# A fused attention and feed-forward kernel on one core: the second half's feature rows transposed by TensorE instead of by DMA, and GpSimd's accumulating transfer issued later in each tile

## The chip, the core and the metric

The kernel runs on one NeuronCore of a Trainium2 chip. Its time is the device time of one execution in microseconds (us); lower is better. Engines are written as in the profile: PE is TensorE's matmuls, PEld its weight loads, DVE is VectorE, ACT is ScalarE, POOL is GpSimd, SP is SyncE, which only issues transfers.

## What is computed

The input `x` is 1024 rows (32 x 32) of 512 values. Cut to what matters:

```python
x = x + attention(conv(x) + context)      # 32 query heads, 8 key/value heads
m = mix(x)                                # per batch element a 32 x 32 mixing matrix and a bias
gate = silu(m @ dequant(gate_w))          # 512 -> 1792
up = m @ dequant(up_w)                    # 512 -> 1792
x = x + (gate * up) @ dequant(down_w)     # 1792 -> 512
```

The weights of the three last products are integers with a scale for each group of 128 rows and each column. The change touches only the feed-forward part, the last 180 us or so; what it calls features is `m`.

## The kernel before

**Stages.** First comes the convolution, then sixteen attention units (8 key/value heads x 2 halves of the rows), each with projections, scores and output products. All products are made in float16 from a high half and a low half of one operand or of both. Then comes the feed-forward part, in which everything is held transposed: channels on partitions, rows along the free axis.

**The feed-forward part.** The 1024 rows are two halves of 512 (`HT`), the 1792 inner channels are 14 blocks of 128 (`IC`). That gives `TILES` = 28 tiles, and tile `n` is block `n % 14` of half `n // 14`. In tile `n` PE runs `gate(n)` (4 banks, each a high and a low product, lines 1037 and 1038), `down(n-2, (0, 1))` (lines 1057 and 1061), `up(n)` (lines 1053 and 1054) and `down(n-2, (2, 3))`. That is 24 matmuls of 128x512 a tile; `down` runs two tiles behind (`LAG` = 2). The order is written out by hand, the same on every engine, and waits are on semaphore counts.

**The other engines in tile n.** ACT and DVE scale the banks of `gate` by the group's scale: ACT writes bank 0 into `whole` and bank 2 into `part`, DVE adds banks 1 and 3 (`scaled`, line 2021). POOL adds `part` to `whole` (`add_part`, line 2284), ACT takes silu of it (line 1447). ACT and DVE make `exact` out of the banks of `up` (lines 1467 and 2032). POOL multiplies (`hidden(n)`, line 2289), ACT makes the high half of the product (`hidden_high`, line 1476), POOL the low half (`hidden_low(n)`, line 2295), and `down(n)` on PE waits for the low half.

**The results of down.** Output blocks 0 and 2 of `down(n)` are added to `acc` by DVE (`down_added_to`, line 2054). Blocks 1 and 3 are scaled by ACT into one of three buffers `dprod` (line 1483), and one transfer issued by POOL adds both to `acc` in memory (`move_down(n)`, line 2307, 512 KB, for `n` = 1 to 24). `move_down(n)` first waits until `move_down(n-1)` has landed (`l_acc`), since both add to the same place. In the POOL program it stands after `hidden` and ahead of `add_part`:

```python
for n in range(LAG, TILES):
    if n > LAG:
        hidden(n - 1)
        move_down(n - 1 - LAG)
    add_part(n)
    hidden_low(n - 1)
```

**The residual.** `x` has to be transposed too. PE turns it in 8 groups of four 128x128 transposes into one bank, `side` (`turn_x`, line 1126): four for half 1 in tiles 9 to 12 (`TURN_X`), copied by ACT into `acc`, and four for half 0 in tiles 16 and 17. The latter DVE adds to half 0's finished `acc` (`result(c)`, line 2071), and SP stores them. `result(1)` waits for the landing of `move_down(13)`, the last of half 0. It stands on DVE between the two `scaled` of tile 17, and `turn_x(0, 2)` on PE waits for it, because it reuses `side`.

**The features.** Half 0's features are transposed by PE at the start of the part. Half 1's are computed during tiles 2 to 4 into `fnat` (4 tiles of 128 rows, rows on partitions). In tiles 5, 7, 9 and 11 (`ROWS`) ACT makes the high half and DVE the low half of one row tile in `fpair` (`rows_high`, line 1429; `rows_low`, line 2013), still with rows on partitions. SP then issues 16 transposing transfers (line 654) into `fT`, which `gate(14)` reads.

**The bound of the hidden values.** For each half a maximum over partitions is broadcast: PE transposes (`hidden_rows`, line 1002), DVE reduces (line 1992) and multiplies a 4x4 identity with it (line 1993, `hdiag`), PE multiplies `spread` with that (`hidden_all`, line 1008). For half 1 it is done in tiles 5 and 6.

**The end.** After the loop `down` of tiles 26 and 27 follows (`last_downs`), DVE adds 6 blocks, of which the first, block 3 of tile 25, waits for the landing of `move_down(24)`, then `hidden_low(27)` and the others; POOL adds four blocks (`add_down`, line 2319), the first of which waits for the same landing.

## Time and profile before

| | us |
|---|---|
| median of 3 executions (lowest, highest) | 681.24 (680.61, 681.83) |
| the profiled execution, its own time | 680.94 |
| its span, first to last instruction | 679.1 |
| PE busy in it | 659.5 |
| DVE, POOL, ACT busy in it | 563.2, 458.5, 411.9 |
| first matmul of the feed-forward part | 500.0 |

The granted TensorE clock is 0.997 on average, which is the 2.4 GHz level. A matmul row of 128x512 is listed with 0.38 us, but the next one starts 0.216 us later; for the pace of PE one reads the distance between starts. In the timeline a row is: start, duration, engine, line, operation, output<-inputs, shape, count, and in brackets how long the engine had been idle before and who ended that.

### The profile page before, as it was taken

What the parts mean: (1) busy time and instruction counts of PE and PEld (TensorE: products, weight loads), DVE (VectorE), ACT (ScalarE), POOL (GpSimd) and SP (SyncE); (2) the same over time, 40 slices, a digit from 0 to 9 for tenths busy, and PEclk for the clock granted to TensorE, in tenths of its full rate; (3) what the DMA queues carried; (4) which work ended last, traced back from release to release, by engine and by line L of the source; (5) the groups of instructions that cost most, each with busy time, mean ns of one, the idle gap of its engine ahead of it and who ended that gap; (6) DMA issues with size and microseconds to landing.
All of it is one profiled execution on the core that took longest, in us unless ns stands there. A gap on an engine that the chain in (4) does not pass through costs nothing.

```text
span 679.1 us, 14435 instructions
## 1 busy us (share of the span) xinstructions
PE 659.5 (97%) x4952; PEld 370.0 (54%) x4952; DVE 563.2 (83%) x870; ACT 411.9 (61%) x1233; POOL 458.5 (68%) x379
## 2 busy tenths in 40 slices
PE   9998999999999999999999999999989999999995
PEld 8855555646566465665656656565644434444441
DVE  4979779879879788987978888777785999899997
ACT  0477663845647384374655638446475778877874
POOL 0367973884685497288659648747537678887886
PEclk9999999999999999999999999999999999999998
DMA  7520157379359348536735943563300156556454
GB/s 262 189 95 1 66 163 140 94 178 183 104 100 270 94 90 268 104 89 158 203 85 106 278 109 77 160 106 102 57 1 0 32 109 124 110 110 139 94 105 113
DMA packets 112672, 82.70 MB, mean 122 GB/s; under 512 B 93264, under 2 KB 93936, under 8 KB 110448
## 3 DMA queue, kind: packets, MB, share of 16 engines
q1 hardware_dynamic: 108736, 69.51, 40.4%
q0 software_dynamic: 3456, 12.58, 9.9%
q8 instruction: 24, 0.39, 0.2%
q14 instruction: 24, 0.20, 0.1%
q10 hardware_dynamic: 432, 0.01, 0.0%
HBM read 48.14 MB, written 2.21 MB: 74 GB/s over the span
## 4 chain that ended last, share of the span: by engine, by line
PE 75%; DVE 8%; POOL 7%; issue 4%; DMA 3%; ACT 2%; SPq 1%; POOLq 0%; DVEq 0%; ACTq 0%
PE bank L677 19%; PE bank L679 18%; PE bank L678 18%; PE bank L1053 2%; PE bank L1054 2%; PE bank L1037 2%; PE bank L1061 2%; PE bank L1038 2%; PE bank L1057 2%; DMA acc<-dprod 2%; POOL wqlo L2156 2%; PE bank L877 1%; DMA wqr<-in_wq 1%; DVE mx L1594 1%; DVE exact L2032 1%
## 5 line engine op out<-in xcount | busy, mean ns | idle before, releaser
L677 PE MATMUL bank<-wohi,oThi 128*128 128x512 f16 x256 | 97.1, 379 | 2.2 <-DVE oTlo L1802 2.1
L677 PE MATMUL bank<-wqhi,cThi 128*128 128x512 f16 x256 | 97.0, 379 | 0.8 <-POOL wqlo L2156 0.6
L678 PE MATMUL bank<-wolo,oThi 128*128 128x512 f16 x256 | 97.0, 379 | 0.0
L679 PE MATMUL bank<-wohi,oTlo 128*128 128x512 f16 x256 | 97.0, 379 | 0.0
L679 PE MATMUL bank<-wqhi,cTlo 128*128 128x512 f16 x256 | 97.0, 379 | 0.0
L678 PE MATMUL bank<-wqlo,cThi 128*128 128x512 f16 x256 | 97.0, 379 | 0.0
L1222 ACT ACTIVATE qraw<-bank 128x512 f32<-128x512 f32 x64 | 37.9, 592 | 82.4 <-PE bank L679 82.1
L2166 POOL TENSOR_TENSOR wolo<-wor,wohi 128x512 f16<-128x512 f32 x32 | 42.6, 1353 | 57.9 <-ACT wohi L1202 57.9
L2204 POOL TENSOR_TENSOR qinv<-qms,neghalf 128x8 f32<-128x8 f32 x28 | 53.6, 1914 | 39.3 <-ACT qms L1241 39.3
L1233 ACT ACTIVATE qsq<-qraw 128x128 f32<-128x128 f32 x256 | 75.5, 302 | 1.7
L677 PE MATMUL bank<-wkvhi,cThi 128*128 128x256 f16 x256 | 69.9, 273 | 0.0
L678 PE MATMUL bank<-wkvlo,cThi 128*128 128x256 f16 x256 | 69.8, 273 | 0.0
L679 PE MATMUL bank<-wkvhi,cTlo 128*128 128x256 f16 x256 | 69.8, 273 | 0.0
L2192 POOL TENSOR_TENSOR qn<-qraw,down 128x512 f16<-128x512 f32 x56 | 66.9, 1195 | 2.8 <-ACT qraw L1222 2.8
L2032 DVE SCALAR_TENSOR_TENSOR exact<-bank,uscl,exact 128x512 f32<-128x512 f32 x84 | 62.7, 747 | 7.2 <-ACT exact L1467 2.9
L2156 POOL TENSOR_TENSOR wqlo<-wqr,wqhi 128x512 f16<-128x512 f32 x32 | 43.3, 1382 | 27.0 <-ACT wqhi L1188 27.0
L1810 DVE SCALAR_TENSOR_TENSOR x<-bank,ysc,x 128x512 f32<-128x512 f32 x64 | 46.1, 743 | 16.3 <-PE bank L679 16.2
L2289 POOL TENSOR_TENSOR whole<-whole,exact 128x512 f32<-128x512 f32 x27 | 36.5, 1350 | 21.4 <-DVE exact L2032 20.2
L1233 ACT ACTIVATION_READ_ACCUMULATOR qsq<-qraw 128x1 f32 x256 | 49.5, 193 | 0.0
L1202 ACT ACTIVATE wohi<-wor 128x512 f16<-128x512 f32 x32 | 17.5, 618 | 48.3 <-DVE wor L1622 48.3
L1759 DVE SCALAR_TENSOR_TENSOR qn<-qraw,qn 128x512 f16<-128x512 f32 x56 | 41.5, 751 | 5.2 <-POOL qn L2192 4.9
L1053 PE MATMUL bank<-fT,uint 128*128 128x512 f16 x112 | 42.5, 380 | 1.7 <-DVE whole L2021 1.4
(231 smaller groups left out, 1806.6 us busy)
## 6 DMA issues: line engine op xcount, KB each, us to landing
acc<-dprod POOLq DMA_DIRECT2D x24, 512.0 KB, 4.6
wqr<-in_wq SPq DMA_DIRECT2D x8, 1024.0 KB, 7.4
wor<-in_wo SPq DMA_DIRECT2D x8, 1024.0 KB, 9.2
raw<-in_gu_w SPq DMA_DIRECT2D x28, 256.0 KB, 3.5
zeros<-in_gu_z SPq DMA_DIRECT2D x28, 256.0 KB, 4.6
wkvr<-in_wkv SPq DMA_DIRECT2D x8, 512.0 KB, 7.2
raw<-in_dn_w SPq DMA_DIRECT2D x14, 256.0 KB, 2.8
zeros<-in_dn_z SPq DMA_DIRECT2D x14, 256.0 KB, 3.5
```

The source lines that it names most:

```text
L677: mm(o, ahi, bhi, start=start and k == 0, stop=False)
L678: mm(o, ahi, blo, start=False, stop=False)
L679: last = mm(o, alo, bhi, start=False, stop=stop and k == n - 1)
L1053: mm(o, uint[:, i, c, :], fThi[:, c, tokens(half)], start=True, stop=False)
L1233: A(qsq[:, t % 2, g, :], qraw[:, t, g, :], ACT.Square, accum_out=qss[:, g, t:t + 1]).then_inc(a_qss, 1)
L1759: V.scalar_tensor_tensor(qpair[:, t, 1, :, :], qraw[:, t, :, :], V_DOWN, qpair[:, t, 0, :, :], ALU.mult, ALU.subtract).then_inc(d_qlo, 1)
L1810: V.scalar_tensor_tensor(x[:, q, :], PC[t][:, :], ysc[:, half:half + 1], x[:, q, :], ALU.mult, ALU.add).then_inc(d_y, 1)
L2032: V.scalar_tensor_tensor(u, up_bank(n, c)[:, :], uscl[:, half, i, c:c + 1], u, ALU.mult, ALU.add).then_inc(d_us, 1)
L2156: Q.tensor_tensor(wqlo[:, c, :], wqr[:, c, :], wqhi[:, c, :], ALU.subtract).then_inc(p_wq, 1)
L2166: Q.tensor_tensor(wolo[:, g, :], wor[:, g, :], wohi[:, g, :], ALU.subtract).then_inc(p_wo, 1)
L2192: Q.tensor_tensor(qpair[:, t, 0, :, :], qraw[:, t, :, :], down[:, :, None].broadcast_to([P, G, HD]), ALU.mult).then_inc(p_qhi, 1)
L2204: Q.tensor_tensor(qinv[:, :, pair], qms[:, :, pair], neghalf[:, :, pair], ALU.pow).then_inc(p_qpow, 1)
```

## The change

It does four things.

1. The four row tiles of half 1's features are transposed by PE from `fnat` (float32) into `side`, by a new function `turn_rows`, in tiles 7, 8, 10 and 12 (`ROWS`). ACT and DVE make the halves out of that bank, straight into `fT`. The 16 transposing transfers of SP and the buffer `fpair` are gone; `gate(14)` waits for DVE's last low half instead.
2. `turn_x` of half 1 moves from tiles 9 to 12 to tiles 9, 11, 13 and 14. The bank `side` is now shared, so each group waits for the reader of the group before.
3. In POOL's loop `move_down(n - 3)` stands behind `hidden_low(n - 1)` instead of ahead of `add_part(n)`, but in the last tile it stays ahead. Its waits are the same.
4. `hdiag` is gone: DVE only reduces, and PE multiplies the broadcast row maximum with the identity. ACT's copy of the result in tile 7 stands earlier.

```diff
-ROWS = (5, 7, 9, 11)
-TURN_X = (9, 10, 11, 12)
+ROWS = (7, 8, 10, 12)
+TURN_X = (9, 11, 13, 14)
...
-            for t in range(HQ):
-                sp.wait_ge(d_fTlo, KC + t + 1)
-                for b in range(BQ):
-                    start = HT + P * t + S * b
-                    sp.dma_start(fT[:, :, :, start:start + S].rearrange("p k c n -> p (k c) n"),
-                                 fpair[S * b:S * b + S, t, :, :, :].rearrange("p k c n -> p (k c) n"),
-                                 transpose=True).then_inc(l_fT, 16)
...
-                pe.wait_ge(d_hdiag, half + 1)
+                pe.wait_ge(d_hrow, half + 1)
...
-                mm(bound_all(), spread[0:MAXIMA, :], hdiag[0:MAXIMA, :], start=True, stop=True).then_inc(t_hx, 1)
+                mm(bound_all(), hrow[0:MAXIMA, :].broadcast_to([MAXIMA, P]), ident[0:MAXIMA, 0:MAXIMA],
+                   start=True, stop=True).then_inc(t_hx, 1)
...
-                        pe.wait_ge(l_fT, 16 * HQ * BQ)
+                        pe.wait_ge(d_fTlo, KC + HQ)
...
-                elif c:
+                elif c == 3:
                     pe.wait_ge(a_xT, c)
                 else:
                     pe.wait_ge(d_y, HQ * UNITS)
-                    pe.wait_ge(a_hm, 2)
+                    pe.wait_ge(d_fTlo, KC + c + 2)
...
+            def turn_rows(t):
+
+                pe.wait_ge(a_fnat, HQ + t + 1)
+                if t == 0:
+                    pe.wait_ge(a_hm, 2)
+                elif t == 1:
+                    pe.wait_ge(d_fTlo, KC + t)
+                else:
+                    pe.wait_ge(a_xT, t - 1)
+                for c in range(KC):
+                    last = nc.tensor.transpose(side[:, P * c:P * c + P], fnat[:, t, P * c:P * c + P], ident)
+                last.then_inc(t_rows, 1)
...
-                    turn_x(1, n - TURN_X[0])
+                    turn_x(1, TURN_X.index(n))
+                elif n in ROWS:
+                    turn_rows(ROWS.index(n))
...
-                act.wait_ge(a_fnat, HQ + t + 1)
-                A(fpair[:, t, 0, :, :], fnat[:, t, :].rearrange("p (c n) -> p c n", n=P), ACT.Copy,
+                act.wait_ge(t_rows, t + 1)
+                A(fThi[:, :, rows(t)], side[:, :].rearrange("p (c n) -> p c n", n=P), ACT.Copy,
...
-                V.scalar_tensor_tensor(fpair[:, t, 1, :, :], fnat[:, t, :].rearrange("p (c n) -> p c n", n=P), fup[:, 1:2],
-                                       fpair[:, t, 0, :, :], ALU.mult, ALU.subtract).then_inc(d_fTlo, 1)
+                V.scalar_tensor_tensor(fTlo[:, :, rows(t)], side[:, :].rearrange("p (c n) -> p c n", n=P), fup[:, 1:2],
+                                       fThi[:, :, rows(t)], ALU.mult, ALU.subtract).then_inc(d_fTlo, 1)
...
             for n in range(LAG, TILES):
                 if n > LAG:
                     hidden(n - 1)
+                if n == TILES - 1:
                     move_down(n - 1 - LAG)
                 add_part(n)
                 hidden_low(n - 1)
+                if LAG < n < TILES - 1:
+                    move_down(n - 1 - LAG)
```

The instruction order of the two kernels at the three places that the prediction speaks of follows. Line numbers of the changed kernel differ a little from those before (POOL: 2295 is `add_part`, 2300 `hidden`, 2306 `hidden_low`, 2318 `move_down`).

POOL, tiles 25 to 27 before (2289 is `hidden`, 2284 `add_part`, 2295 `hidden_low`, 2307 `move_down`, 2319 `add_down`), from `hidden(25)` on:

```order
L2289 TENSOR_TENSOR whole<-whole,exact 128x512
L2307 DMA acc<-dprod 128x1024
L2284 TENSOR_TENSOR whole<-whole,part 128x512
L2295 TENSOR_TENSOR hT<-whole,hT 128x512
L2289 TENSOR_TENSOR whole<-whole,exact 128x512
L2307 DMA acc<-dprod 128x1024
L2284 TENSOR_TENSOR whole<-whole,part 128x512
L2295 TENSOR_TENSOR hT<-whole,hT 128x512
L2319 TENSOR_TENSOR acc<-acc,dprod 128x512 x4
```

POOL at the same place of the changed kernel:

```order
L2300 TENSOR_TENSOR whole<-whole,exact 128x512
L2295 TENSOR_TENSOR whole<-whole,part 128x512
L2306 TENSOR_TENSOR hT<-whole,hT 128x512
L2318 DMA acc<-dprod 128x1024
L2300 TENSOR_TENSOR whole<-whole,exact 128x512
L2318 DMA acc<-dprod 128x1024
L2295 TENSOR_TENSOR whole<-whole,part 128x512
L2306 TENSOR_TENSOR hT<-whole,hT 128x512
L2330 TENSOR_TENSOR acc<-acc,dprod 128x512 x4
```

`move_down(23)` has moved behind two compute instructions, `move_down(24)` has stayed, and only `hidden(26)` is left between them. In tiles 4 to 26 the pattern is that of the first four rows.

DVE before, from the end of tile 5 into tile 6 (2013 is `rows_low`, 1992 and 1993 the reduction and `hdiag`, 2021 `scaled`):

```order
L2054 SCALAR_TENSOR_TENSOR acc<-bank,dsc,acc 128x512
L2032 SCALAR_TENSOR_TENSOR exact<-bank,uscl,exact 128x512
L2013 SCALAR_TENSOR_TENSOR fpair<-fnat,fup,fpair 128x512
L1992 TENSOR_REDUCE hrow<-bank 4x1
L1993 SCALAR_TENSOR_TENSOR hdiag<-const,hrow 4x4
L2021 SCALAR_TENSOR_TENSOR whole<-bank,gscl,whole 128x512
```

DVE at the same place of the changed kernel:

```order
L2065 SCALAR_TENSOR_TENSOR acc<-bank,dsc,acc 128x512
L2043 SCALAR_TENSOR_TENSOR exact<-bank,uscl,exact 128x512
L2006 TENSOR_REDUCE hrow<-bank 4x1
L2032 SCALAR_TENSOR_TENSOR whole<-bank,gscl,whole 128x512
L2032 SCALAR_TENSOR_TENSOR part<-bank,gscl,part 128x512
```

Two instructions have left the stretch ahead of tile 6's first `scaled`; `rows_low` stands in tile 7 for the first time.

PE in the changed kernel, in the middle of tile 7 (1054 and 1058 are `down`, 1136 is `turn_rows`, 1050 and 1051 are `up`):

```order
L1054 MATMUL bank<-hT,dints 128x512
L1058 MATMUL bank<-hT,dints 128x512
L1136 MATMUL bank<-const,fnat 128x128 x4
L1050 MATMUL bank<-fT,uint 128x512
L1051 MATMUL bank<-fT,uint 128x512
```

Before there was nothing between `down` and `up` in tiles 7, 8, 13 and 14, and `turn_x` in tiles 9 to 12; now each of the tiles 7 to 14 has one group of four transposes there.

## Rows read from the trace of the kernel before

**Rows 1.** The page, part 1: busy us (share of the span) and instructions.
```profile
PE 659.5 (97%) x4952; PEld 370.0 (54%) x4952; DVE 563.2 (83%) x870; ACT 411.9 (61%) x1233; POOL 458.5 (68%) x379
```

**Rows 2.** Timeline of PE, first matmuls of tiles 15 and 16.
```profile
597.14 0.38 PE L1037 MATMUL bank<-fT,gint 128*128 128x512 f16 x1
...
602.32 0.38 PE L1037 MATMUL bank<-fT,gint 128*128 128x512 f16 x1
```

**Rows 3.** Timeline of PE, tile 6: its first matmul, a stall in `up`, tile 7's first.
```profile
544.54 0.38 PE L1037 MATMUL bank<-fT,gint 128*128 128x512 f16 x1
...
547.35 0.38 PE L1054 MATMUL bank<-fT,uint 128*128 128x512 f16 x1
548.78 0.39 PE L1053 MATMUL bank<-fT,uint 128*128 128x512 f16 x1 [1.05 <-DVE whole L2021]
...
551.13 0.38 PE L1008 MATMUL bank<-hdiag,spread 4*128 4x4 f32 x2
551.45 0.39 PE L1037 MATMUL bank<-fT,gint 128*128 128x512 f16 x1
```

**Rows 4.** Timeline of DVE, end of tile 5 and start of tile 6.
```profile
546.18 0.74 DVE L2013 SCALAR_TENSOR_TENSOR fpair<-fnat,fup,fpair 128x512 f16<-128x512 f32 x1
546.84 0.27 DVE L1992 TENSOR_REDUCE hrow<-bank 4x1 f32<-4x128 f32 x1
547.14 0.92 DVE L1993 SCALAR_TENSOR_TENSOR hdiag<-const,hrow 4x4 f32<-4x4 f32 x1
547.99 0.73 DVE L2021 SCALAR_TENSOR_TENSOR whole<-bank,gscl,whole 128x512 f32<-128x512 f32 x1
```

**Rows 5.** Timeline of PE, a group of transposes in tile 9.
```profile
564.78 0.60 PE L1126 MATMUL bank<-const,x 128*128 128x128 f32 x4
565.21 0.38 PE L1053 MATMUL bank<-fT,uint 128*128 128x512 f16 x1
```

**Rows 6.** Timeline of PE, a stall in tile 14.
```profile
591.68 0.38 PE L1038 MATMUL bank<-fT,gint 128*128 128x512 f16 x1
593.22 0.39 PE L1057 MATMUL bank<-hT,dints 128*128 128x512 f16 x1 [1.16 <-POOL hT L2295]
```

**Rows 7.** Chain of waits, 580 to 594 us: start, us, what.
```profile
582.81 6.51 DMA acc<-dprod
...
589.87 0.04 POOL acc L2307
```

**Rows 8.** The page, part 6: POOL's transfers, KB each, median us to landing.
```profile
acc<-dprod POOLq DMA_DIRECT2D x24, 512.0 KB, 4.6
```

**Rows 9.** Timeline of POOL, tile 16: `move_down(13)`, `add_part(16)`, `hidden_low(15)`.
```profile
605.52 0.88 POOL L2307 DMA_DIRECT2D acc<-dprod  x1
606.14 1.57 POOL L2284 TENSOR_TENSOR whole<-whole,part 128x512 f32<-128x512 f32 x1
607.38 1.45 POOL L2295 TENSOR_TENSOR hT<-whole,hT 128x512 f16<-128x512 f32 x1
```

**Rows 10.** Timeline of DVE: the second `scaled` of tile 16, and `result(1)` in tile 17.
```profile
605.11 0.74 DVE L2021 SCALAR_TENSOR_TENSOR part<-bank,gscl,part 128x512 f32<-128x512 f32 x1
...
610.52 0.68 DVE L2071 TENSOR_TENSOR acc<-bank,acc 128x512 f32<-128x512 f32 x1
```

**Rows 11.** Timeline of PE, tile 17: its first matmul, and `turn_x(0, 2)`.
```profile
608.38 0.38 PE L1037 MATMUL bank<-fT,gint 128*128 128x512 f16 x1
...
611.35 0.63 PE L1126 MATMUL bank<-const,x 128*128 128x128 f32 x4 [0.22 <-DVE acc L2071]
```

**Rows 12.** Timeline of POOL from `hidden_low(25)` to the end.
```profile
661.77 1.45 POOL L2295 TENSOR_TENSOR hT<-whole,hT 128x512 f16<-128x512 f32 x1
664.32 1.28 POOL L2289 TENSOR_TENSOR whole<-whole,exact 128x512 f32<-128x512 f32 x1 [1.10 <-DVE exact L2032]
665.54 0.88 POOL L2307 DMA_DIRECT2D acc<-dprod  x1
...
670.18 5.76 POOL L2319 TENSOR_TENSOR acc<-acc,dprod 128x512 f32<-128x512 f32 x4 [1.35 <-DMA acc<-dprod]
```

**Rows 13.** Busy time by stretch; columns: us, busy PE, PEld, DVE, ACT, POOL, PEclk, DMA share, GB/s.
```profile
673.00:679.00 6.00, 0.10 (x1) 0.00 (x0) 2.38 (x4) 0.17 (x1) 2.66 (x3) 0.67 0.47 175
```

More of the change, by code:

```diff
@@ L262, in build @@
         between = sb("between", [P, 5 * DM + 40], F32, ffn)
-        fpair = sb("fpair", [P, HQ, 2, KC, P], F16, ffn)
+        between2 = sb("between2", [P, HQ, 2, KC, P], F16, ffn)
         dprod3 = sb("dprod3", [P, 2, HT], F32, ffn)
@@ L393, in build @@
         d_fTlo = sem("d_fTlo")
-        l_fT = sem("l_fT")
+        t_rows = sem("t_rows")
         t_g = sem("t_g")
@@ L408, in build @@
         d_hx = sem("d_hx")
-        d_hdiag = sem("d_hdiag")
+        d_hrow = sem("d_hrow")
         t_hx = sem("t_hx")
@@ L461, in tokens, with rows @@
             return slice(HT * half, HT * half + HT)
+        def rows(t):
+            return slice(HT + P * t, HT + P * t + P)
         def up_bank(n, c):
@@ L1525, in _ @@
                 scaled(n, 2)
+                if n == 7:
+                    hidden_scale(1)
                 if n >= LAG:
@@ L1533, in _ @@
                     rows_high(ROWS.index(n))
-                if n == 7:
-                    hidden_scale(1)
-                elif n in TURN_X:
-                    turned_x(n - TURN_X[0])
-                elif n == IC - 1:
+                if n in TURN_X:
+                    turned_x(TURN_X.index(n))
+                if n == IC - 1:
                     later_scales()
@@ L1988, in hidden_bound, with hidden_maxima @@
                 V.tensor_reduce(hx[:, 0:1], fmx[:, half, 0:HQ], AX_X, ALU.max).then_inc(d_hx, 1)
-            def hidden_diagonal(half):
+            def hidden_maxima(half):
                 dve.wait_ge(t_hx, 2 * half + 1)
-                link(V.tensor_reduce(hrow[0:MAXIMA, :], bound_rows(half), AX_X, ALU.max))
-                V.scalar_tensor_tensor(hdiag[0:MAXIMA, :], ident[0:MAXIMA, 0:MAXIMA], TOP,
-                                       hrow[0:MAXIMA, :].broadcast_to([MAXIMA, MAXIMA]), ALU.mult,
-                                       ALU.mult).then_inc(d_hdiag, 1)
+                if half:
+                    dve.wait_ge(t_hx, 2)
+                V.tensor_reduce(hrow[0:MAXIMA, :], bound_rows(half), AX_X, ALU.max).then_inc(d_hrow, 1)
             def hidden_power(half):
@@ L2078, in _ @@
             mix_power(0)
-            hidden_diagonal(0)
+            hidden_maxima(0)
             probs_low(UNITS - 1)
@@ L2102, in _ @@
                 elif n == 6:
-                    hidden_diagonal(1)
+                    hidden_maxima(1)
                 elif n == 9:
```

## The prediction, made before the changed kernel ran

> **What bounds the kernel now.** I read the page first: PE is busy for 97% of the span [rows 1]. So the sum has to be made of PE's time: what instructions it gains or loses, and where it waits. Next I read the timeline of PE in the feed-forward part, since the change touches nothing ahead of it except one small DVE instruction. The pace is the distance between the first matmuls of two tiles. In tile 15, which has nothing but its 24 matmuls, it is 602.32 - 597.14 = 5.18 us [rows 2], and that is 24 times 0.216. This is the floor of a tile. Then I looked for the tiles that are longer than the floor plus their extra instructions, and asked at each what came last:
>
> - Tile 6 takes 551.45 - 544.54 = 6.91 us. In `up` PE stands still from 547.35 to 548.78, 1.21 us more than the normal distance, and DVE's `scaled` releases it [rows 3]. DVE is late because `rows_low`, the reduction and `hdiag` stand ahead of that `scaled`, from 546.18 to 547.99 [rows 4].
> - Tile 14 has a stall of 593.22 - 591.68 - 0.22 = 1.32 us, released by POOL's low half [rows 6]. The chain of waits says why: a transfer of `move_down` took 6.51 us to land instead of the median 4.6 [rows 7, 8], POOL could issue the next only at 589.87, and `add_part` and `hidden_low` stood behind it. SP's transposing transfers were under way at that time.
>
> From tile 6 to tile 14 PE spends 597.14 - 544.54 = 52.60 us [rows 2, 3].
>
> **The change, part by part.**
>
> *Transposes on PE, and the stalls they replace.* A group of four float32 transposes moves the next matmul by 565.21 - 564.78 = 0.43 us [rows 5]. Half 1's residual groups are only moved within tiles 7 to 14; four groups are new, +1.72 us. After the change each of the tiles 7 to 14 has exactly one group. If no stall is left, tiles 6 to 14 take 9 x 5.18 + 8 x 0.43 = 50.06, and the broadcast product at tile 6's end keeps its 551.45 - 551.13 = 0.32 [rows 3]: 50.38 us, or 2.2 less than the 52.60 of before. So this part **gains 2.2 us net**: 1.7 paid, 3.9 of stalls removed (1.2 in tile 6, 1.3 directly in tile 14, the rest small ones, also from late row halves and late transfers). Does it really leave no stall? Three things have to hold.
>
> First, tile 6: without `rows_low` and `hdiag` the `scaled` can start when the reduction ends, at 546.18 + 0.3 instead of 547.99, and done 0.7 later it is ahead of PE's demand at 547.57. Second, DVE in a row tile has 8 large instructions at the pace of 0.66 us (546.18 to 546.84 [rows 4]), 5.3 us; a tile now lasts 5.18 + 0.43 = 5.61, so DVE does not fall behind, which it did when row tiles had no group on PE. Third, the shared bank: in tiles 8, 9, 11 and 13 PE waits for the DVE part of the group before. DVE ends it 546.84 - 544.54 = 2.3 us after the next tile's first matmul [rows 3, 4]; PE wants the bank after 12 matmuls, 12 x 0.216 = 2.6 us. It is just in time, by 0.3 us. I cost it at nothing; if the cover is gone, up to 0.5 at each of four places.
>
> ACT and DVE make the same number of halves as before, from the bank instead of from memory; DVE's `scaled`, which reads a bank, is listed with 0.73 us and `rows_low` with 0.74 [rows 4], so this costs nothing. SP has nothing else to do while it issues the 16 transfers, so their removal frees no one but the DMA queues. `hdiag` of half 0 stands in a chain of DVE work at 498 us ahead of `gate(0)`; I take 0.15 us off for it, between 0 and the 0.9 of rows 4.
>
> *`move_down` behind the low half.* On POOL `add_part` and `hidden_low` no longer stand behind the issue (605.52 to 606.14 [rows 9], 0.62 us) and its wait. PE paces all tiles, so that is worth only the stalls counted above. But the transfer now starts later, and the landing has readers. Most have tiles of slack: the next `move_down` has a tile of 5.18 us against 4.6 of landing plus 0.54 until POOL goes on (582.81 + 6.51 = 589.32, issue at 589.87 [rows 7]), 5.14 in all, which just fits. Two readers have none.
>
> (a) *Tile 17.* `result(1)` waits for the landing of `move_down(13)`. Before it was issued at 605.52 [rows 9] and landed 4.6 later [rows 8], at 610.1; DVE came to `result(1)` at 610.52 [rows 10], 0.4 us after it. Now the order is `add_part(16)`, `hidden_low(15)`, then the transfer. `add_part(16)` cannot start before DVE's `scaled` of tile 16 ends, 605.11 + 0.74 = 605.85 [rows 10]. It takes 607.38 - 606.14 = 1.24 [rows 9], so the low half starts at about 607.15. The low half takes between 1.24 (the same size) and its listed 1.45. The transfer is issued at 608.4 to 608.6 and lands at 613.0 to 613.2. `result(1)` starts 2.5 to 2.7 us later than before, and so does `turn_x(0, 2)` on PE, which was already released by it with 0.22 us of idle [rows 11]. Behind it PE's `up(17)` is queued, behind `result(1)` on DVE the second `scaled` of tile 17. Everything shifts, and as later tiles are at the floor nothing gives it back: **+2.6 us**.
>
> (b) *The end.* `move_down(24)` keeps its place, but waits for `move_down(23)`, which is now issued behind `hidden_low(25)`. That started at 661.77 [rows 12] and can be at most 0.15 earlier; with 1.24 to 1.45 for it the issue is at 662.9 to 663.2, the landing 4.6 later at 667.5 to 667.8, and POOL goes on 0.54 later, at 668.0 to 668.3 instead of 665.54 [rows 12]: 2.4 to 2.8 us. Queued behind it are `add_part(27)` and `hidden_low(26)`, for which PE's last `down` waits, and its landing, for which DVE's first added block and POOL's first of four adds wait, at 670.18 before. The four adds took 5.76 us though 4 x 1.27 = 5.1 would do, so up to 0.4 can come back. I take **+2.3**, bounds 1.9 and 2.8.
>
> How a page stands to that: the Trainium skill (DMA: Bandwidth & Descriptors, the two cost components) fits a transfer's time as 2.0 us plus its bytes at 436 GB/s. For 512 KB that would be an estimated 3.2 us, and the two waits would come out 1.3 us shorter each. The trace disagrees, the median row is 4.6 for this accumulating transfer, and the sum goes by the row.
>
> *Sum.* -2.2 - 0.15 + 2.6 + 2.3 = +2.55 us. The profiled execution of before took 680.94, so 683.5 by its own time; the median of the runs, 681.24, is 0.3 above it, and I give **683.8 us** for the median.
>
> **The rivals.** A measurement of this kernel can tell about 0.2% from no change: 1.36 us, so "same" is 679.9 to 682.6.
>
> 1. *Faster: the later landings are never waited for.* Then only -2.35 is left, 678.9 us. It decides at tile 17: the landing must be there by 610.5 in the old timeline, so the issue by 605.9. But the low half ahead of it starts at 607.15 by rows 9 and 10. Only if POOL's chain ran much ahead of DVE could it be, and DVE's `scaled` binds it. Chance 0.06.
> 2. *Only one of the two waits is paid in full*, because a slack I did not see takes the other, or both land about 1.2 us sooner. Then -2.35 + 2.5 gives about 681.4, no change. For it: SP's transfers are gone, which stretched landings to 6.51. Against it: the median was undisturbed already. Chance 0.13.
> 3. *The shared bank.* The row part on DVE comes after PE's demand at four places. With 0.3 to 0.5 us each that is 1.2 to 2.0 more: 685.0 to 685.8. The margin is 0.3 us, but DVE was late there before for a cause that is removed. Chance 0.07.
> 4. *The clock.* In tile 17 PE now stands still for 0.4 + 2.6 = 3 us, twice its longest pause in this part. After its last matmul the mean granted clock of the last 6 us is 0.67 [rows 13], so it does fall to the 1.2 GHz level when PE has no work. Were it to fall in tile 17, each following tile would take 10.4 instead of 5.18 as long as it lasts: 686 or more. Chance 0.04. The Trainium skill (TensorE: Matmul & The Clock Gate, why this matters for your kernels) warns that idle gaps of PE in mid-kernel can bring it back to the lower clock. The trace shows pauses of up to 1.3 us [rows 6] without that and no longer one, so it stays a small chance.
>
> **How the numbers follow.** The forecast has 0.70, on its own 682.9 to 684.8 by the bounds of (a) and (b) and 0.5 for what I leave out. The range has to take in most of rival 2 and the start of rival 3: 681.2 to 685.3 leaves out rival 1, part of 2 and 3, and 4, some 0.18. Slower by over 0.2% is the forecast but for its low edge (0.68), rivals 3 and 4: 0.79 with rounding. Same is rival 2 and that edge, 0.14. Faster is rival 1 and a little more, 0.07.
>
> **What would show it.** In the changed profile: no stall in `up` of tile 6; 5.61 us a tile from 7 to 14, and about 50.4 us from tile 6's to tile 15's first matmul; four new groups of 0.43. In tile 17 a gap on PE of some 3 us ahead of `turn_x(0, 2)`, behind it DVE's `result(1)` with about 2.5 us of idle time that ends with a DMA landing. In the last tile POOL idle for about 2.4 us ahead of `move_down(24)`, released by the DMA. I am wrong if `result(1)` has no idle time, if the last `move_down` is issued within 1 us of the end of `hidden(26)`, or if tiles 8, 9, 11 and 13 are longer than 5.7 us.

## The result, and the profile after

The change makes the kernel slower: 687.04 us (686.72 to 687.99) against 681.34 us of the kernel before, a ratio of 1.0072 with the interval 1.0044 to 1.01. The forecast was 683.8 us, its range ended at 685.3. The direction was right, the size was not. (The ratios here and in the table below are those of the measurement; the quotient of two medians can differ from them by about 0.1%.) The rest speaks of the profiled execution of after, 686.72 us with a span of 684.9, beside before's span of 679.1: 5.8 us more.

The page after, answering to [rows 1] (PE's busy time, and the granted clock in 40 slices, whose last one is 7 tenths, before 8):

```profile
PE 662.8 (97%) x4968; PEld 374.6 (55%) x4968; DVE 562.0 (82%) x868; ACT 413.6 (60%) x1233; POOL 456.7 (67%) x379
...
PEclk9999999999999999999999999999999999999997
```

PE's busy share is 97% as before, so the loss must be looked for by stretches. Busy time by windows, for after; the windows are tile 6 to tile 14, tiles 15 and 16, tile 17 in two pieces, tiles 18 to 26, and the end:

```profile
core 0: us, PE busy (x) PEld busy (x) DVE busy (x) ACT busy (x) POOL busy (x), PEclk, DMA share, GB/s
545.56:596.32 50.76, 50.76 (x252) 24.65 (x250) 46.52 (x72) 43.61 (x76) 41.54 (x41) 1.00 0.50 94
596.32:607.56 11.24, 11.24 (x58) 5.64 (x57) 10.60 (x17) 9.17 (x16) 9.41 (x9) 1.00 0.54 107
607.56:613.72 6.16, 2.75 (x15) 1.10 (x12) 2.90 (x5) 2.51 (x4) 2.32 (x3) 0.95 0.51 107
613.72:618.57 4.85, 4.85 (x21) 2.71 (x22) 3.73 (x6) 1.96 (x4) 2.86 (x3) 0.71 0.29 110
618.57:665.19 46.62, 46.62 (x219) 21.13 (x217) 42.84 (x64) 39.06 (x63) 39.55 (x36) 1.00 0.55 108
665.19:684.90 19.71, 10.74 (x41) 4.08 (x39) 12.82 (x18) 7.00 (x12) 11.39 (x10) 0.82 0.43 107
```

The same three stretches of before (tiles 6 to 14, tile 17, the end):

```profile
544.54:597.14 52.60, 50.04 (x236) 22.27 (x234) 47.37 (x73) 42.59 (x74) 43.15 (x41) 1.00 0.60 110
608.38:614.84 6.46, 6.24 (x35) 3.21 (x33) 5.88 (x10) 4.60 (x8) 4.96 (x5) 1.00 0.72 175
661.99:679.10 17.11, 9.66 (x41) 3.49 (x39) 12.87 (x19) 7.33 (x12) 11.07 (x10) 0.88 0.45 115
```

That gives the account of the 5.8 us:

| stretch | before | after | difference | forecast |
|---|---|---|---|---|
| up to tile 6's first matmul | 544.54 | 545.56 | +1.02 | -0.15 |
| tiles 6 to 14 | 52.60 | 50.76 | -1.84 | -2.2 |
| tiles 15 and 16 | 11.24 | 11.24 | 0 | 0 |
| tile 17 | 6.46 | 11.01 | +4.55 | +2.6 |
| tiles 18 to 26 | 47.15 | 46.62 | -0.53 | 0 |
| the end | 17.11 | 19.71 | +2.60 | +2.3 |

**Tile 17.** PE's timeline answers to [rows 11]: it stands still 3.57 us longer than the normal 0.22 from one start to the next (609.93 to 613.72), and behind that its matmuls come 0.43 us apart instead of 0.22 until 616.30.

```profile
609.93 0.38 PE L1058 MATMUL bank<-hT,dints 128*128 128x512 f16 x1
613.72 1.08 PE L1123 MATMUL bank<-const,x 128*128 128x128 f32 x4 [3.41 <-DVE acc L2082]
614.60 0.63 PE L1050 MATMUL bank<-fT,uint 128*128 128x512 f16 x1
615.02 0.63 PE L1051 MATMUL bank<-fT,uint 128*128 128x512 f16 x1
...
616.30 0.48 PE L1050 MATMUL bank<-fT,uint 128*128 128x512 f16 x1
616.62 0.38 PE L1051 MATMUL bank<-fT,uint 128*128 128x512 f16 x1
```

A spacing twice as long is the 1.2 GHz level; the granted clock of that window was 0.71. It costs 0.45 in the transposes (0.88 instead of 0.43) and 0.94 in the five matmul distances from 614.60 to 616.62 (2.02 instead of 1.08): 1.39 us. DVE and POOL show who is waited for, as in [rows 9, 10]: `result(1)` waits for a landing, and that transfer was issued at 608.22.

```profile
612.88 0.69 DVE L2082 TENSOR_TENSOR acc<-bank,acc 128x512 f32<-128x512 f32 x1 [3.15 <-DMA acc<-dprod]
```

```profile
603.15 0.88 POOL L2318 DMA_DIRECT2D acc<-dprod  x1 [1.02 <-DMA acc<-dprod]
603.76 1.58 POOL L2300 TENSOR_TENSOR whole<-whole,exact 128x512 f32<-128x512 f32 x1
605.00 1.58 POOL L2295 TENSOR_TENSOR whole<-whole,part 128x512 f32<-128x512 f32 x1
606.45 1.24 POOL L2306 TENSOR_TENSOR hT<-whole,hT 128x512 f16<-128x512 f32 x1
608.22 0.88 POOL L2318 DMA_DIRECT2D acc<-dprod  x1 [0.53 <-ACT dprod L1495]
```

`move_down(12)` was issued at 603.15, not because of the low half, but because it waited for the landing before it, and landed at 607.68. POOL issued the next 0.54 later. The low half in front of it ended at the same moment, 606.45 + 1.24 = 607.69.

**The end.** POOL's timeline answers to [rows 12]. Its first add comes at 675.97, before at 670.18, 5.79 later, of which 3.20 were there at the last tile's first matmul (665.19 against 661.99) and 2.59 are new. From that add to the end of the span it is 8.93 us, before 8.92, so PE's lower clock in this stretch (0.82, before 0.88) costs nothing here.

```profile
666.26 0.88 POOL L2318 DMA_DIRECT2D acc<-dprod  x1 [0.44 <-ACT dprod L1495]
667.18 1.27 POOL L2300 TENSOR_TENSOR whole<-whole,exact 128x512 f32<-128x512 f32 x1
671.33 0.88 POOL L2318 DMA_DIRECT2D acc<-dprod  x1 [2.88 <-DMA acc<-dprod]
671.93 1.56 POOL L2295 TENSOR_TENSOR whole<-whole,part 128x512 f32<-128x512 f32 x1
673.15 1.45 POOL L2306 TENSOR_TENSOR hT<-whole,hT 128x512 f16<-128x512 f32 x1
675.97 5.75 POOL L2330 TENSOR_TENSOR acc<-acc,dprod 128x512 f32<-128x512 f32 x4 [1.37 <-DMA acc<-dprod]
```

### The profile page after: what moved, and what is told of

Read it like the earlier page. It is cut to its first block and busy times, and to the rows that moved or that the text cites. A ratio compares the mean times of both kernels' runs of the same rounds, so it can differ in the third digit from the quotient of the medians.

```text
span 684.9 us, 14456 instructions
## 1 busy us (share of the span) xinstructions
PE 662.8 (97%) x4968; PEld 374.6 (55%) x4968; DVE 562.0 (82%) x868; ACT 413.6 (60%) x1233; POOL 456.7 (67%) x379
## 5 line engine op out<-in xcount | busy, mean ns | idle before, releaser
L1495 ACT ACTIVATE dprod<-bank,dsc 128x512 f32<-128x512 f32 x52 | 35.7, 686 | 18.1 <-PE bank L1058 17.0
L1058 PE MATMUL bank<-hT,dints 128*128 128x512 f16 x112 | 42.5, 388 | 3.3 <-POOL hT L2306 3.3
```

Of the source, the lines that this page charges most:

```text
L1058: mm(down_bank(n, c)[:, :], dints[:, n % IC, P * c:P * c + P], hTlo[:, n % (LAG + 1), :], start=False, stop=True).then_inc(t_dn, 1)
```

## The experiments

Theory A says that the place of `move_down` costs all of the loss, by two waits for a landing and by the clock behind the first. Its rivals are: the transposes on PE; POOL's order itself rather than the landings; another cause of the low clock. Each comparison stands beside runs of the kernel before on the same chip, whose median was 681.34 to 681.9 us.

| run | us | ratio to before | 95% interval |
|---|---|---|---|
| changed kernel | 687.04 | 1.0072 | 1.0044 to 1.01 |
| `move_down` in the old place | 678.87 | 0.9962 | 0.9946 to 0.9979 |
| before, new place alone | 690.5 | 1.0123 | 1.0091 to 1.0154 |
| old place in tile 16 only | 687.53 | 1.0073 | 1.0044 to 1.0101 |
| old place in tile 26 only | 688.48 | 1.0098 | 1.0068 to 1.0127 |
| pause filled with matmuls | 684.35 | 1.0037 | 1.0024 to 1.0051 |
| half the bytes | 679.79 | 0.9964 | 0.9945 to 0.9983 |
| between add and low half | 688.68 | 1.01 | 1.0084 to 1.0116 |
| half 0's results a tile later | 682.3 | 1.0 | 0.9986 to 1.0015 |
| before, without `hdiag` | 680.41 | 0.9965 | 0.9947 to 0.9983 |
| old place, results later | 679.73 | 0.9971 | 0.9953 to 0.9989 |
| results later, old place from tile 18 | 681.37 | 0.9991 | 0.9974 to 1.0009 |

**The old place, with all the rest of the change.**

```diff
                 if n > LAG:
                     hidden(n - 1)
-                if n == TILES - 1:
+                if n > LAG:
                     move_down(n - 1 - LAG)
                 add_part(n)
                 hidden_low(n - 1)
-                if LAG < n < TILES - 1:
-                    move_down(n - 1 - LAG)
```

> The changed kernel with `move_down` back in its old place (right behind `hidden`, ahead of `add_part`) in every tile; the transposes on PE, the missing `hdiag` and the rest stay. Theory A (the two waits on late landings, and the clock that fell behind the first, cost all of it): no gap over 1 us on PE in tile 17, POOL goes on with the last transfer without a wait of 2.9 us, tiles 6 to 14 stay at about 50.8 us; the time is the changed kernel's less 4.5 and less 2.6, 679.9 us, 1.2 to 1.8 below the kernel before. Theory B (the transposes on PE and the shared bank cost the time): the time stays above 684. Theory C (without the new place the low half is late in the tiles 6 to 14): stalls of 1 us come back there and the time is 681 to 682.

Measured: 678.87 us, 0.38% below before. The windows of tiles 6 to 14, tile 17 and the end of this run:

```profile
544.36:595.12 50.76, 50.76 (x252) 24.61 (x250) 46.53 (x72) 43.59 (x76) 41.47 (x41) 1.00 0.50 95
606.36:612.76 6.40, 6.24 (x34) 3.20 (x32) 6.18 (x11) 4.58 (x8) 4.93 (x5) 1.00 0.72 176
661.93:679.20 17.27, 9.49 (x41) 3.57 (x39) 12.64 (x18) 7.33 (x12) 11.02 (x10) 0.91 0.44 112
```

Theory A holds and B falls: tiles 6 to 14 are as quick as in after, tile 17 and the end as short as before. C falls too, the low half is not late in tiles 6 to 14. So the parts of the change that gain are those on PE and DVE, and the new place costs 1.0072 - 0.9962 = 1.1%, 7.5 us.

The old place is not free, though. The profiled execution was the slowest of the twelve, 681.05 us, and in it tile 26 takes 7.26 us, 2.08 more than the floor: POOL waited for a landing of 6.7 us (issued at 647.42), the add and the low half stood behind that wait, and PE waited for the low half. The same happened in tile 14 of before; here no transposing transfer was under way.

```profile
654.68 0.88 POOL L2318 DMA_DIRECT2D acc<-dprod  x1 [2.03 <-DMA acc<-dprod]
656.53 1.44 POOL L2306 TENSOR_TENSOR hT<-whole,hT 128x512 f16<-128x512 f32 x1
658.03 0.39 PE L1054 MATMUL bank<-hT,dints 128*128 128x512 f16 x1 [1.47 <-POOL hT L2306]
```

**The new place alone.** The kernel before, on POOL:

```diff
                 if n > LAG:
                     hidden(n - 1)
+                if n == TILES - 1:
                     move_down(n - 1 - LAG)
                 add_part(n)
                 hidden_low(n - 1)
+                if LAG < n < TILES - 1:
+                    move_down(n - 1 - LAG)
```

> The kernel before with one part of the change alone: `move_down(n - 3)` behind `hidden_low(n - 1)`, the last tile excepted. Theory A: tile 17 takes 9.5 to 11 us with a gap of over 3 us on PE, with the clock at its lower level behind it, and the last tile is about 2.5 us longer: 681.3 + 4.5 + 2.5 = 688.3 us, less up to 1.3 for the stall of tile 14, so 687 to 688.5. Theory B (the waits need the transposes on PE to become long): 681 to 683.

Measured: 690.5 us, slower than the changed kernel and above what either theory gave. The two long tiles are there (10.34 us and an end of 20.92), and a third one that I had not foreseen, tile 9 with 9.39 us. POOL's and DVE's timelines there (POOL first):

```profile
564.53 0.88 POOL L2307 DMA_DIRECT2D acc<-dprod  x1 [1.35 <-DMA acc<-dprod]
565.14 0.50 POOL L2345 TENSOR_TENSOR ht<-hm 128x1 f32<-128x1 f32 x1
565.71 0.19 POOL L2347 TENSOR_TENSOR ht<-ht 128x1 f32<-128x1 f32 x1
565.98 0.19 POOL L2349 TENSOR_TENSOR ht<-ht,hm 128x1 f32<-128x1 f32 x1
...
566.21 0.15 DVE L2001 TENSOR_SCALAR hdown<-ht 128x1 f32<-128x1 f32 x1 [2.65 <-POOL ht L2349]
```

`hidden_product(1)` stands behind tile 8's `move_down` on POOL. That waits for a landing of 5.3 us, beside SP's transposing transfers, and DVE's `hidden_power(1)`, with all of DVE's queue behind it, waits for the product. PE then stood still for 2.3 us and its clock fell there as well (0.84 over the tile). In the changed kernel the transposing transfers are gone and tile 9 takes 5.85. The two parts of the change so depend on each other: the new place is worse with the old transfers.

**One tile's place alone, 16 or 26.** The condition of the first, and of the second:

```diff
-                if n == TILES - 1:
+                if n in (IC + LAG, TILES - 1):
                     move_down(n - 1 - LAG)
...
-                if n == TILES - 1:
+                if n >= TILES - 2:
                     move_down(n - 1 - LAG)
```

with the tiles named left out of the condition behind `hidden_low`.

> The changed kernel with `move_down(13)` alone, in tile 16, ahead of `add_part`. Theory A1 (the low half and the add in front of that one transfer make it late, as the prediction had it): it is issued at about 605, lands at 610, tile 17 takes 6.5 us and the time is 687.0 - 4.5 = 682.5. Theory A2 (the chain of transfers makes it late: in the changed kernel the landing of `move_down(12)` came at 607.68 and POOL went on 0.54 later): it is issued at 608.2 as before, POOL's `add_part(16)` and `hidden_low(15)` now stand behind it, PE's gap in tile 17 keeps its 3.8 us and the time is 687 or up to 1.5 more.

> The changed kernel with `move_down(23)` alone, in tile 26, ahead of `add_part`. Theory A1 (its own place makes the end late): it is issued at about 664.9 instead of 666.3, lands at 669.5, the last `move_down` follows 1.3 us sooner, and with it the four adds: 687.0 - 1.3 = 685.7. Theory A2 (the whole chain of transfers since tile 17 runs one issue late: `move_down(22)` landed at 665.72): the issue is at 666.26 in any case, `add_part(26)` and `hidden_low(25)` come behind it, and the time stays within 0.5 us of 687.0 or gets longer.

Measured: 687.53 and 688.48 us, no gain from either. POOL in tile 16 of the first:

```profile
602.86 0.88 POOL L2318 DMA_DIRECT2D acc<-dprod  x1 [1.05 <-DMA acc<-dprod]
603.47 1.59 POOL L2300 TENSOR_TENSOR whole<-whole,exact 128x512 f32<-128x512 f32 x1
607.93 0.88 POOL L2318 DMA_DIRECT2D acc<-dprod  x1 [2.87 <-DMA acc<-dprod]
608.53 1.56 POOL L2295 TENSOR_TENSOR whole<-whole,part 128x512 f32<-128x512 f32 x1
```

A2 holds in both. In the first the transfer is issued where it was, 0.55 us after the landing before it; moved forward it only makes the add and the low half wait too, and PE stands still in two places (2.3 and 1.4 us). In the second `move_down(23)` is bound by the landing before it in the same way (POOL idle for 2.46 us ahead of the issue at 665.10), and PE stands still for 2.1 us in the last tile for the low half. Its profiled execution, 685.54 us, was the fastest of six, and its time alone would have spoken for A1. This corrects my reason for (a): the low half in front of the one issue (in after it ended at 607.69, the landing came at 607.68) is not the only thing that makes it late; a chain of transfers in which each waits for the last does it by itself. The second profile shows this without a stretched landing: the transfer before was issued at 660.00, so the moved one could not come ahead of 665.10, and at the new place it would have come only some 0.1 us later (an estimate: the two issues before lie 5.24 us apart). One link takes 4.53 + 0.54 = 5.07 us of a tile's 5.18. A stretched landing, such as the 5.85 us of the transfer issued at 596.76, is given back at 0.1 us a tile (0.5 in a row tile). At the old place the chain runs two POOL instructions earlier, 1.27 for the add and 1.24 for the low half, so it can be 2.5 us ahead of where it is now, and that is the reserve that the change gave away.

**The pause filled.** In tile 17, ahead of `turn_x`:

```diff
                 elif n in (IC + LAG, IC + LAG + 1):
+                    if n == IC + LAG + 1:
+                        pe.wait_ge(a_g, 2 * n + 1)
+                        for _ in range(15):
+                            mm(up_bank(n, 0)[:, :], uint[:, n % IC, 0, :], fThi[:, 0, tokens(1)], start=True, stop=True)
                     turn_x(0, 2 * n - 2 * IC - 2 * LAG)
```

> The changed kernel with 15 more matmuls on PE in tile 17 (15 x 0.216 = 3.24 us), in front of `turn_x(0, 2)`, so that PE works through most of the pause of 3.57 us; their product lands in the bank that `up(17)` overwrites afterwards, so nothing of the result changes. The waits stay as they are. Theory A (the pause lets the clock fall, and that costs 1.4 us behind it): no low clock behind tile 17, distances of 0.22 us in `up(17)` at once, tile 17 takes 9.6 us instead of 11.0 and the time is 687.0 - 1.4 = 685.6. Theory B (the low clock in tile 17 has another cause): it comes in this tile all the same, PE does the 15 matmuls and the time is 687 or above.

Measured: 684.35 us, though PE does 3.2 us more work. Its timeline, with the fillers in one row:

```profile
609.70 3.40 PE L1173 MATMUL bank<-fT,uint 128*128 128x512 f16 x15
613.21 0.63 PE L1123 MATMUL bank<-const,x 128*128 128x128 f32 x4
613.68 0.38 PE L1050 MATMUL bank<-fT,uint 128*128 128x512 f16 x1
613.89 0.38 PE L1051 MATMUL bank<-fT,uint 128*128 128x512 f16 x1
```

The clock stays up (1.00 over the tile), the tile takes 9.59 us instead of 11.01, 1.42 less. That is theory A, by the two profiles: with the pause filled the clock does not fall, and its fall cost 1.4 of the 4.55 us; the wait cost the other 3.15. The median fell by 2.7, more than this tile, but the two intervals overlap (1.0024 to 1.0051 and 1.0044 to 1.01); in the profiled execution it was 0.45 earlier already at tile 17's first matmul, and its end was 0.5 shorter.

**Half the bytes.**

```diff
-                    pool.dma_start(acc[:, half, 2:KC, :],
-                                   moved_blocks(n)[:, :, :], accum_op=ALU.add).then_inc(l_acc, 16)
+                    pool.dma_start(acc[:, half, 2:3, :],
+                                   moved_blocks(n)[:, 0:1, :], accum_op=ALU.add).then_inc(l_acc, 16)
```

> The changed kernel with half of each accumulating transfer left out: 256 KB, block 2 of the down product, where 512 KB with blocks 2 and 3 were moved; block 3's sums of 24 tiles are missing from the result. Landing bounded by 2.3 (half of 4.5) and 4.5 us; I take 3.3. Theory A (what is waited for is the landing): `result(1)` and the last `move_down` wait about 1.2 us less each, and each next transfer has 1.2 us of slack, so that a stretched one no longer makes the next one late; tile 17 takes 8 to 9.5 us, the end is 1.2 to 2.4 shorter, in all 682.5 to 684.5. Theory B (POOL's order alone, add and low half ahead of the issue, costs it, whatever is moved): 686.5 to 687.5.

Block 3 of the down product is left out of the transfers, so the result is not the kernel's. Measured: 679.79 us, faster than before and below what either theory gave, with POOL's order unchanged. The median landing came after 3.3 us. `result(1)` still waits, but 1.22 us instead of 3.15, and the last `move_down` 1.14 instead of 2.88. PE's pause in tile 17 is 1.6 us and the clock stays up; tile 17 takes 7.72 us, the end 17.06. B is refuted. I had put the gain too low: the clock's 1.4 us was not in my sum for it, and the end came back whole.

**Between the two places.**

```diff
                 add_part(n)
-                hidden_low(n - 1)
                 if LAG < n < TILES - 1:
                     move_down(n - 1 - LAG)
+                hidden_low(n - 1)
```

> The changed kernel with `move_down` between `add_part` and `hidden_low` in tiles 3 to 26, halfway between the old place and the new. Theory A2 (the chain of transfers runs with no slack at the new place; each is 1.24 us earlier here): the landing of `move_down(13)` comes at 611 to 611.5 in the changed kernel's time, PE's gap in tile 17 is 1.3 to 2.3 us instead of 3.57, the clock stays up behind it (no longer gap than 1.3 us was without effect in the kernel before), and the end is 1.2 shorter: 687.0 - 1.9 - 1.4 - 1.2 = 682.5, between 681.0 and 684. Theory B (any place behind `add_part` is as bad): over 686.

Measured: 688.68 us (the profiled execution, 691.36, was the slowest of four), as slow as theory B gave it, but for another reason than the landings alone. PE's pause in tile 17 did shrink, to 2.7 us, but its landing was a stretched one (5.17) and the clock fell. The main loss is new: tiles 19 to 26 take mostly 5.66 us each instead of 5.18. ACT, DVE and POOL there:

```profile
654.53 1.46 POOL L2306 TENSOR_TENSOR hT<-whole,hT 128x512 f16<-128x512 f32 x1
...
656.08 0.69 ACT L1454 ACTIVATE whole<-bank,gscl 128x512 f32<-128x512 f32 x1 [0.87 <-POOL hT L2306]
...
656.87 0.75 DVE L2032 SCALAR_TENSOR_TENSOR whole<-bank,gscl,whole 128x512 f32<-128x512 f32 x1 [0.76 <-ACT whole L1454]
```

`whole` may be written again only when the low half has read it. So low half, ACT's `scaled`, DVE's `scaled` twice, `add_part` and again the low half make a loop. With the issue of 0.61 us inside (653.92 to 654.53) it takes 5.66 us; without it I estimate 5.66 - 0.61 = 5.05, just under a tile. The new place keeps the issue out of this loop, and so does the old one, where it lies ahead of `add_part` while that waits for DVE anyway: there most tiles take 5.18 us.

**The reader a tile later.** The four groups of `turn_x(0, ..)` and the four `result` blocks stand in tiles 17 to 19 instead of 16 to 18, for instance on PE:

```diff
-                elif n in (IC + LAG, IC + LAG + 1):
-                    turn_x(0, 2 * n - 2 * IC - 2 * LAG)
+                elif n in (IC + LAG + 1, IC + LAG + 2):
+                    turn_x(0, 2 * n - 2 * IC - 2 * LAG - 2)
```

> The changed kernel with its transfers where they are, but the four residual groups and `result` blocks of half 0 one tile later (tiles 17 and 18 instead of 16 and 17), so that the landing of `move_down(13)` has a tile of 5.18 us more before its reader. Theory A (the landing is late only against this reader): no gap over 1 us in tiles 16 to 18, no low clock there, tile 17 and 18 take 6.05 us each; the end keeps its wait: 687.0 - 4.5 = 682.5. Theory B (the later transfer delays something else there too, the bank `side` or POOL): a gap of over 1 us in tile 18 or 19, time above 684.

Measured: 682.3 us, as expected. The tiles 17 and 18 take 6.06 and 6.41 us (6.05 expected for both), the clock stays at 1.00, `result` no longer waits for a landing; only the end keeps its wait and is even longer than in after, 20.76 us against 19.71, since the chain of landings is later still: `move_down(24)` is issued 7.20 us behind the last tile's first matmul instead of 6.14. The transfers are where the change put them: the late landing costs time only where someone reads it.

**`hdiag` alone**, taken out of the kernel before.

```diff
-                link(V.tensor_reduce(hrow[0:MAXIMA, :], bound_rows(half), AX_X, ALU.max))
-                V.scalar_tensor_tensor(hdiag[0:MAXIMA, :], ident[0:MAXIMA, 0:MAXIMA], TOP,
-                                       hrow[0:MAXIMA, :].broadcast_to([MAXIMA, MAXIMA]), ALU.mult,
-                                       ALU.mult).then_inc(d_hdiag, 1)
+                V.tensor_reduce(hrow[0:MAXIMA, :], bound_rows(half), AX_X, ALU.max).then_inc(d_hdiag, 1)
```

> The kernel before with one part of the change alone: `hdiag` is no longer made, PE multiplies the broadcast maxima by the identity. Theory A (in tile 6 `hdiag` and `rows_low` together made `scaled` late, as the prediction had it): `scaled` starts 0.85 us sooner, the stall of 1.21 us in `up(6)` shrinks to 0.3 to 0.5, tile 6 takes 6.1 instead of 6.91, and half 0's `hdiag` at 498 us brings 0.15 more: 681.3 - 0.9 = 680.4. Theory B (`rows_low` alone makes tile 6 late, or what is gained is lost at the next stall): tile 6 keeps over 6.7 us, the time stays at 681.3.

Measured: 680.41 us, ratio 0.9965. Tile 6 takes 5.94 instead of 6.91 and its stall is 0.25 us. DVE's `scaled` starts at once behind the reduction:

```profile
545.86 0.74 DVE L2013 SCALAR_TENSOR_TENSOR fpair<-fnat,fup,fpair 128x512 f16<-128x512 f32 x1
546.52 0.27 DVE L1995 TENSOR_REDUCE hrow<-bank 4x1 f32<-4x128 f32 x1
546.72 0.73 DVE L2021 SCALAR_TENSOR_TENSOR whole<-bank,gscl,whole 128x512 f32<-128x512 f32 x1
```

This is A, and it says that of the 1.2 us in tile 6 `hdiag` alone made 0.96. In this profile most of that is lost again at the next stalls, as B had it for all of it: tiles 6 to 14 take 52.30 us against 52.60. Tile 14 keeps its stall of the kernel before (it takes 7.05 us here, with a landing of 7.24 beside SP's transposing transfers).

**Combinations.** Late results together with the old place in every tile (first edit on POOL), or from tile 18 on (second):

```diff
-                if n == TILES - 1:
+                if n > LAG:
                     move_down(n - 1 - LAG)
...
-                if n == TILES - 1:
+                if n > IC + LAG + 1:
                     move_down(n - 1 - LAG)
```

> Both cures at once: `move_down` in its old place in every tile, and the results of half 0 one tile later. In the old place the reader in tile 17 cost 6.41 - 6.05 = 0.36 us. Theory A (with each landing in time nothing is left there): tiles 17 and 18 take 6.05 each, the time is 678.9 - 0.36 = 678.5, and a measurement can hardly tell it from the old place alone. Theory B (the later results collide with something else): over 679.5.

> The changed kernel with both waits taken away but the new place kept where no reader is near: results of half 0 one tile later, `move_down` behind the low half in tiles 3 to 17 and in its old place from tile 18 on. Theory A (the new place is harmless away from its readers, and brings nothing): 682.3 of the late reader, less 2.3 for the end, 680.0, at best the 678.9 of the old place everywhere. Theory C (the new place brings something in the tiles 6 to 14): under 678.5.

Measured: 679.73 and 681.37 us. The first can't be told from the old place alone (the intervals 0.9953 to 0.9989 and 0.9946 to 0.9979 overlap), so moving the results as well brings nothing that shows. By my expectation's own bound, over 679.5, it even falls to theory B, and tile 18 takes 6.51 us and not 6.05: the reader's 0.36 us is not gained, it moves with the reader. The second has its end at 16.9 us, as short as the old place, but it stays 1.4 us above the 680.0 of theory A: where the place changes over, in tile 19, POOL's add and low half come to stand behind the wait of the late chain (2.89 us of idle time on POOL), and the tile takes 7.24 us. Keeping the new place in tiles 3 to 17 brought nothing (tiles 6 to 14 are again 50.8 us). The lowest median is that of the changed kernel with `move_down` in its old place everywhere, 678.87 us. But by the ratios it can't be told from the kernel before without `hdiag` (0.9962 and 0.9965). What the transposes on PE add to that, 1.5 us in tiles 6 to 14 (50.76 against 52.30), shows in the profiles only, and there the second has an unusually long landing in tile 14.

## Why the prediction was wrong

Of the 5.8 us, 2.55 were forecast. The other 3.25 are 1.95 in tile 17, 1.17 ahead of tile 6, 0.36 in tiles 6 to 14 and 0.3 at the end, less 0.53 in tiles 18 to 26.

1. **The PE part was right.** Tile 6 has no stall in `up`, the row tiles take 5.62 us (5.61 forecast), four new groups of 0.43, and no wait for the shared bank. Forecast -2.2, found -1.84; the missing part is mostly tile 9 with 5.85 us. That is longer than the 5.7 I had named as a sign of being wrong, but it is not rival 3: the transposes start at 564.98, the normal 0.22 behind the matmul ahead of them, and the time is lost in `up`, where DVE's `scaled` comes behind three small instructions of `hidden_power(1)` (564.72 to 565.16). With the old place the two gaining parts gave 2.6 us in the medians, 2.35 forecast. How that divides between them is open, since `hdiag` alone gives nearly the same ratio.
2. **The end came out in size**, +2.3 forecast, +2.6 found, and the waits are those named, but partly by luck. I let `hidden_low(25)` set the issue of `move_down(23)`. In after it ended at 665.82, but POOL issued at 666.26, 0.54 behind a landing at 665.72: the chain of landings set it. And of the up to 0.4 us that the four adds could have given back nothing came: they take 5.75 us as before.
3. **The step that failed is (a), tile 17**: +2.6 forecast, +4.55 found. Two things were missing. The larger is the clock, 1.4 us. I had named it as rival 4 and gave it 0.04 because "the trace shows pauses of up to 1.3 us [rows 6] without that and no longer one". That a trace holds no longer pause says nothing of what a longer one does; [rows 13] was the only row on a longer one, and there the clock did fall. The price belonged into the sum of the forecast, since the forecast itself made the pause of 3 us. The rule of the Trainium skill that I cited (TensorE: Matmul & The Clock Gate, why this matters for your kernels), that idle gaps in mid-kernel can bring the lower clock back, is what the run with the filled pause shows, with 1.42 us. The price I named with the rival, following tiles of 10.4 us, was too high: the low level lasted for the transposes and five matmul distances.
4. The smaller is the issue of `move_down(13)`. I let the low half alone set it, 608.4 to 608.6 with tile 17 beginning at 608.38, so 0.1 us behind it. In after tile 17 began at 607.56 and the low half ended 0.13 behind that, as forecast; but the landing of `move_down(12)` came only then, at 607.68, and POOL takes 0.54 from a landing it waits for to the next issue, so the issue came 0.66 behind. PE's wait is 0.6 us longer for it: 2.6 + 0.6 + 1.4 = 4.6. I had written that landing and tile "just fit", 5.14 against 5.18, and did not ask what one stretched landing does with a reserve of 0.04. The landing of 5.85 us issued at 596.76 was still not given back two tiles later.
5. **Outside the sum**: +1.02 at tile 6's first matmul, where -0.15 was forecast. Some 0.6 of it was there at `gate(0)`; the code ahead of it is the same but for the `hdiag` instruction of half 0 (PE's wait there fell from 0.88 to 0.69 us, about the 0.15 forecast), and in the profiled executions of the other versions `gate(0)` lies between 499.2 and 500.9. Another 0.45 is a stretch behind 500.6 us with a granted clock of 0.63 in its first 4.4 us. It is in the profiles of four other versions too (new place alone, old place in tile 26 only, pause filled, between) and not in those of the rest or of before. What makes it fall there is open. The 0.53 us gained in tiles 18 to 26 were small stalls, which are gone.

One number beside the sum was off as well: with a landing of 3.2 us in place of 4.6 each wait would be 1.4 us shorter, not 1.3.

## What to carry to other kernels

When an edit delays a transfer, look for the whole chain: who reads the landing, whether the next transfer waits for it, and how much the period of that chain lies under the period of the loop; a chain that fits with 0.1 us to spare hardly gives a stretched landing back. The other place has its price too: ahead of the add and the low half, the wait for a stretched landing holds PE (2.08 us in tile 26 of the profile with the old place). Price a forecast pause of PE with what the clock takes behind it, above all if it is longer than any in the trace. And test the parts of a combined edit apart: here the parts on PE and DVE gained 2.6 us and the new place cost three times that.

## What the hardware showed unexpectedly

- **The price of an accumulating transfer.** 512 KB landed after 4.5 us and 256 KB after 3.3 us (medians), both in 144 packets. The difference, 256 KB in 1.2 us, is some 220 GB/s, which leaves about 2.1 us fixed; this is an estimate from two sizes. The Trainium skill (DMA: Bandwidth & Descriptors, anatomy of one DMA, the two cost components) has nearly the same fixed cost, 2.0 us, but twice the rate, 436 GB/s. For these accumulating transfers the runs speak for half of that.
- **What stretches a landing when no other transfer runs.** Of the 24 landings in after, 15 had no packet of an instruction load beside them, and these took 4.50 to 4.58 us but for the first, 4.74. Nine had one, and four of those took 4.79 to 5.85. The queues of the longest:

```profile
q0 software_dynamic: 144, 0.52, 48.0%
q8 instruction: 1, 0.02, 1.1%
issues: line engine op xcount, KB each, median us to landing
acc<-dprod POOLq DMA_DIRECT2D x1, 512.0 KB, 5.9
```

  That the load of instructions is the cause was not tried; they only coincide. The longest landing of the old place, 6.7 us, had one such packet and no other transfer beside it. In before the two landings with four transposing transfers and no such packet beside them took 5.4 and 5.3 us, and the 6.51 us of [rows 7] had both beside it. So the prediction's reading of that landing, that SP's transfers stretched it, names only one of two candidates.
- **The clock and pauses of PE.** Less the normal 0.22 us, single pauses of 1.3 us (before), 1.6 us (half the bytes; old place) and 2.1 us (old place in tile 26 only) were followed by full clock in these profiles. Those of 2.3 and 2.9 (new place alone), 2.7 (between), 3.4 (old place in tile 26 only, tile 17) and 3.6 us (after) were followed by distances of 0.43 us, the 1.2 GHz level, the one of 2.3 only behind the third matmul. A pause is not the only occasion: at 500 us the level was low in five profiles with no pause of over 0.7 us ahead of it in after.
